# A six-layer graph-attention kernel: layer 1's input transposed into a bank of layer 0, its full copy placed behind the soft maximum

## The reference, cut to what matters

```python
# layer 0
q, k, v = x @ Wq + bq, x @ Wk + bk, x @ Wv + bv          # 8 heads of 32
attn = softmax(where(adj == 0, -inf, q k^T * scale))
x = layernorm((attn v) @ Wo + bo + x) * gamma + beta
# layer 1
sc = where(adj == 0, -inf, (x @ Wq) (x @ Wk)^T / 16)
x = layernorm(x + (softmax(sc) (x @ Wv)) @ Wo + bo) * gamma + beta
# layers 2 to 5
s = where(adj == 0, -1e10, (x Wq^T + bq) (x Wk^T + bk)^T / sqrt(128))
x = layernorm(x + (softmax(s) x) Wc^T) * g + b
```

## Time and profile before

| what | value |
|---|---|
| median of 3 runs | 2370.72 us (2369.71 to 2372.63) |
| the profiled execution | 2373.87 us, of which the span from first to last instruction is 2372.1 us |
| PE busy | 2259.9 us, 95% of the span |
| VectorE, ScalarE, GpSimd busy | 75%, 68%, 76% |
| granted TensorE clock | 0.99 of full |

### The profile page before, as it was taken

The page is one execution under the profiler, slowest core; times in us unless marked ns, Lnnn a source line. Parts: engine busy times, 40 slices in busy tenths (PEclk is TensorE's granted clock), DMA queues, the critical chain, the costliest instruction groups (busy, mean ns, idle before and its releaser), DMA issues.

```text
span 2372.1 us, 59576 instructions
## 1 busy us (share of the span) xinstructions
PE 2259.9 (95%) x20624; PEld 2136.2 (90%) x20624; DVE 1783.3 (75%) x7734; ACT 1620.0 (68%) x5515; POOL 1794.9 (76%) x2399
## 2 busy tenths in 40 slices
PE   6899999999999999999999999999999999999985
PEld 5799999999999999999999999999999999999974
DVE  4777777777877877877877877877777777777864
ACT  5667767767767767767767767766766766767742
POOL 3368878878878878878878878878878878878751
PEclk9999999999999999999999999999999999999998
DMA  4000000100110000010010000000010010000000
GB/s 154 20 23 24 30 28 24 30 28 25 29 28 25 29 28 26 28 28 26 28 28 27 27 28 28 26 28 28 26 28 28 26 28 28 26 29 17 15 10 14
DMA packets 38747, 68.78 MB, mean 29 GB/s; under 512 B 4400, under 2 KB 12848, under 8 KB 37936
## 3 DMA queue, kind: packets, MB, share of 16 engines
q1 hardware_dynamic: 38448, 64.97, 9.0%
HBM read 48.18 MB, written 16.78 MB: 27 GB/s over the span
## 4 chain that ended last, share of the span: by engine, by line
PE 80%; DVE 9%; ACT 7%; issue 2%; POOL 1%; DMA 0%; POOLq 0%; SPq 0%; DVEq 0%
PE value_bank L450 17%; PE qk_bank L442 16%; PE context_bank L595 9%; PE unit_bank L450 7%; PE unit_bank L442 7%; PE qk_bank L549 7%; PE score_bank L579 5%; ACT probs L676 5%; PE unit_bank L506 4%; PE unit_bank L518 3%; DVE scores L820 2%; PE score_bank L576 2%; PE score_bank L586 2%; DVE xT_lo L854 2%; DVE scores L860 1%
## 5 line engine op out<-in xcount | busy, mean ns | idle before, releaser
L1046 POOL TENSOR_TENSOR x<-y,rows 128x512 f32<-128x512 f32 x305 | 392.0, 1285 | 188.9 <-DVE y L913 188.9
L698 ACT CAST xT_hi<-qk_bank 128x512 fp32r<-128x512 f32 x320 | 187.7, 587 | 399.8 <-PE qk_bank L549 399.6
L676 ACT ACTIVATE probs<-scores,negmax 128x128 f32<-128x128 f32 x1024 | 399.1, 393 | 88.6 <-DVE negmax L820 88.6
L913 DVE TENSOR_SCALAR y<-y,mv,rstd 128x256 f32<-128x256 f32 x730 | 304.2, 459 | 191.6 <-POOL rstd L1030 191.3
L442 PE MATMUL qk_bank<-xT_hi,w_lo 128*128 128x256 f32 x1280 | 411.5, 321 | 21.6 <-DVE xT_lo L854 21.3
L1054 POOL TENSOR_TENSOR x<-x,rows 128x512 f32<-128x512 f32 x305 | 393.8, 1291 | 19.2
L450 PE MATMUL value_bank<-w_lo,xT_hi 128*128 128x256 f32 x1280 | 394.4, 308 | 0.0
L442 PE MATMUL qk_bank<-xT_lo,w_hi 128*128 128x256 f32 x1280 | 363.5, 284 | 0.0
L442 PE MATMUL qk_bank<-xT_hi,w_hi 128*128 128x256 f32 x1280 | 362.1, 283 | 0.0
L450 PE MATMUL value_bank<-w_hi,xT_lo 128*128 128x256 f32 x1280 | 361.8, 283 | 0.0
L450 PE MATMUL value_bank<-w_hi,xT_hi 128*128 128x256 f32 x1280 | 361.0, 282 | 0.0
(11 more groups left out here) (93 smaller groups left out, 6503.3 us busy)
## 6 DMA issues: line engine op xcount, KB each, us to landing
x0T<-xT_in SPq DMA_DIRECT2D x64, 256.0 KB, 3.0
x<-x_in SPq DMA_DIRECT2D x64, 256.0 KB, 3.0
out<-x_out SPq DMA_DIRECT2D x64, 256.0 KB, 2.3
adj<-adj_in SPq DMA_DIRECT2D x64, 128.0 KB, 2.2
late_weights<-w_in SPq DMA_DIRECT2D x2, 1024.0 KB, 7.1
rows<-rows_in SPq DMA_DIRECT2D x1, 1792.0 KB, 11.7
probs0T<-w_in SPq DMA_DIRECT2D x4, 256.0 KB, 4.2
x<-w_in SPq DMA_DIRECT2D x1, 1024.0 KB, 13.2
```

Source lines behind the costliest of these rows:

```text
L676: e = act.activation(probs0[:, j, g, quad], scores0[:, j, g, quad], ACT.Exp, scale=-1.0, bias=negmax0[:, j, g, quad:quad + 1], accum_out=t ...
L913: m = dve.tensor_scalar(y[:, r, g], y[:, r, g], mv[:, r, g, 0:1], rstd[:, r, g:g + 1], ALU.subtract, ALU.mult)
L1046: pool.tensor_tensor(result(norm), y[:, NORM_AT[norm] % YS], row_of_each(f"gamma{layer}"), ALU.mult).then_inc(zg_ready, 1)
```

## The change

Layer 1's x (of every group but group 0) is transposed into `unit_bank[0]` in place of `qk_bank`. TensorE waits there for `row_max0(g+1, 0)` and no longer for `move_qk(5g-1)`. ScalarE's full copy `xT` becomes a step of its own, `move_xT`, behind `softmax(5g-1)`, and waits until `xT_lo` is made; VectorE's `split_lo` waits for `xT_hi` alone. `project_qk(5g)` gets a wait for `qk_ready` of the item before, and `transpose_probs0(., 0)` one for the full copy.

```diff
--- before.py
+++ after.py
@@ -371,6 +371,10 @@
             else:
                 engine.wait_ge(x_ready, RESULT_AT[norm] + 1)
 
+        def xT_bank(i):
+
+            return unit_bank[0] if item(i)[0] == 1 and NTH[i] > 0 else qk_bank
+
         block = ctx.enter_context(nc.Block())
 
         @block.sync
@@ -501,6 +505,9 @@
                 if group == 0 and j == 0:
                     pe.wait_ge(eye_loaded, 16)
                 pe.wait_ge(probs0_ready, after_unit(group, j))
+                if j == 0 and group > 1:
+
+                    pe.wait_ge(xT_ready, group)
                 for g in range(G):
                     for quad in range(QUADS):
                         t = pe.transpose(unit_bank[j][:, (g * QUADS + quad) * N:(g * QUADS + quad + 1) * N],
@@ -542,11 +549,14 @@
             def transpose_x(i):
                 layer, group = item(i)
                 wait_result(pe, source_of(i))
-                if NTH[i] > 0:
+                psum = xT_bank(i)
+                if psum is not qk_bank:
+                    pe.wait_ge(negmax0_ready, after_unit(min(group + 1, GROUPS - 1), 0))
+                elif NTH[i] > 0:
                     pe.wait_ge(qk_ready, NTH[i])
                 for kd in range(KD):
                     for g in range(G):
-                        t = pe.transpose(qk_bank[:, (kd * G + g) * N:(kd * G + g + 1) * N],
+                        t = pe.transpose(psum[:, (kd * G + g) * N:(kd * G + g + 1) * N],
                                          x[:, group % HELD, g, kd * P:(kd + 1) * P], eye[:, :])
                 t.then_inc(xT_in_psum, 1)
 
@@ -554,6 +564,10 @@
                 layer, group = item(i)
                 parts = [("scores1", 0), ("scores1", P)] if layer == 1 else [(f"wqT{layer}", 0), (f"wkT{layer}", 0)]
                 pe.wait_ge(xT_lo_ready, after(i))
+                if xT_bank(i) is not qk_bank:
+                    pe.wait_ge(qk_ready, NTH[i])
+                elif layer == 1:
+                    pe.wait_ge(xT_ready, group + 1)
                 project(qk_bank, xT_hi[:, ring(i)], xT_lo[:, ring(i)], parts).then_inc(qk_in_psum, 1)
 
             def project_v(i, g):
@@ -695,9 +709,12 @@
                 act.wait_ge(xT_in_psum, after(i))
                 if NTH[i] >= RING:
                     act.wait_ge(v_in_psum, after(i) - RING)
-                act.copy(flat3(xT_hi[:, ring(i)]), qk_bank[:, :]).then_inc(xT_hi_ready, 1)
-                if layer == 1:
-                    act.copy(flat3(xT[:, :]), qk_bank[:, :]).then_inc(xT_ready, 1)
+                act.copy(flat3(xT_hi[:, ring(i)]), xT_bank(i)[:, :]).then_inc(xT_hi_ready, 1)
+
+            def move_xT(i):
+
+                act.wait_ge(xT_lo_ready, after(i))
+                act.copy(flat3(xT[:, :]), xT_bank(i)[:, :]).then_inc(xT_ready, 1)
 
             def move_qk(i):
                 layer, group = item(i)
@@ -756,6 +773,8 @@
                         split_first(name)
                 if item(i - 1):
                     softmax(i - 1)
+                if item(i) and item(i)[0] == 1:
+                    move_xT(i)
                 if item(i - 1) and late_values(i - 1):
                     move_v(i - 1)
                 if (group := due(i, 6)) is not None:
@@ -845,13 +864,8 @@
                 dve.reciprocal(rtotal[:, small(i)], total[:, small(i)]).then_inc(rtotal_ready, 1)
 
             def split_lo(i):
-                layer, group = item(i)
-                if layer == 1:
-
-                    dve.wait_ge(xT_ready, group + 1)
-                else:
-                    dve.wait_ge(xT_hi_ready, after(i))
-                dve.tensor_tensor(flat3(xT_lo[:, ring(i)]), qk_bank[:, :], flat3(xT_hi[:, ring(i)]).bitcast(F32),
+                dve.wait_ge(xT_hi_ready, after(i))
+                dve.tensor_tensor(flat3(xT_lo[:, ring(i)]), xT_bank(i)[:, :], flat3(xT_hi[:, ring(i)]).bitcast(F32),
                                   ALU.subtract).then_inc(xT_lo_ready, 1)
 
             def row_max(i):
```

## The result

The changed kernel takes 2356.62 us (median of 4 runs, 2355.78 to 2359.72) against 2371.68 (2369.71 to 2373.13): ratio 0.9939, 95% interval 0.9922 to 0.9957. That is 15 us less, 0.24 us for each of 62 groups. Forecast were 9.3 us and 0.15. The sign and the range of 2354 to 2370 held. The narrower range of the forecast itself, 2358 to 2364, was missed: the size was too small by more than a third.

What follows compares the result with a forecast made beforehand. TensorE, busy 95% of the span, was taken as the bound. `xT_lo` starting earlier gave 62 x 0.15 = 9.3 us, other terms nothing: 2370.7 - 9.3 = 2361.4 us; range 2354 to 2370, the forecast's own 2358 to 2364.

Steps and rivals of the forecast that it cites:

- The stall and what was awaited: TensorE's transposes of layer 1's x: x comes 0.50 us before `kT`, so only that much of the stall can go.
- The scores' start: `score(5g-1)` on TensorE, waiting for `kT`, starts at about 1205.48 in place of 1205.94: 0.46 us won per group.
- `xT_lo`'s start: On VectorE, `xT_lo` starts at row_max's end, 1207.10 in place of 1207.25: 0.15 us per group.
- Which of them decides: At `project_qk(5g)`, `xT_lo` sets the gain, 0.15 us per group; the other 0.3 becomes a TensorE wait.
- PE's own path: From the scores to `project_qk(5g)`, TensorE alone could start at 1207.33, winning up to 0.66 us per group.
- The moved copy costs nothing: ScalarE's list behind `softmax(5g-1)` runs 0.48 us later, but slack and idle times absorb it: cost set at nothing.
- The slack: Behind the moved copy, `xT_hi(5g+1)` has 0.06 us to spare before `xT_lo(5g+1)` must start to keep the gain.
- Rival 3: Slower: moved copy delays `xT_hi(5g+1)` on ScalarE; 0.9 us lateness costs 12 us, giving 2383 us. Chance 8%.
- Rival 1: The whole stall at the transposes goes: 0.46 to 0.66 us per group, 29 to 41 us, 2330 to 2342. Chance 5%.
- the rule on banks: Skill's advice to rotate matmul groups through PSUM banks; by it alone the transposes' whole stall, 48.7 us, would go.
- The new waits of TensorE: Added waits in `project_qk(5g)`, `transpose_probs0` and the context: cost zero, at most 0.10 us if one falls on `xT_lo`.

Runs made afterwards that it cites:

- exp_halves: Changed kernel, with ScalarE taking two of the four exponentials of `exp0(g+1, 0)` only after q, k and `probsT` of slot 5g-1: 2356.31 us.
- lo_first: Changed kernel, with VectorE making `xT_lo` of layer 1 ahead of `row_max` of the item before: 2414.86 us.
- bank_only: Changed kernel, with the full copy put back directly behind `xT_hi` and `xT_lo` waiting for it; only the new bank stays: 2352.58 us.
- wait_kept: Changed kernel, with layer 1's transposes in the new bank also waiting for `qk_ready`, as before the change: 2364.28 us.
- copy_late: Changed kernel, with one extra copy of `xT` into a spare tile on ScalarE, behind `move_probsT` in slot 5g: 2381.09 us, ratio 1.0030 to the kernel before.
- copy_twice: Changed kernel, with a second full copy of the bank, into a spare tile, in `move_xT`: 2408.16 us, ratio 1.0159 to the kernel before.

## Why the prediction was right, and where its size was off

**The stall and what was awaited: right.** x came 0.5 us before `kT`, and the transposes start 0.1 us after GpSimd (1195.92 + 1.29 = 1197.21, transposes at 1197.27). With x where it is, no more of that stall can go.

**The scores' start: mis-sized, 0.46 against 0.23.** The prediction let the scores wait for `kT` alone. `score` waits for `probsT` of the item before as well, which ScalarE makes directly behind `kT`. That wait had been hidden under the transposes, so the list of before has it 4 times with 1.4 us in total; the code shows it (`probsT_ready` in `score`), and so does the row of the timeline before that stands behind `kT`:

```profile
1205.23 0.36 ACT L727 COPY probsT<-score_bank 128x256 f32<-128x256 f32 x1
```

It ends at 1205.59, and the scores start 0.12 us behind it after the change, at 1205.71 in the clock of before. It is the wait that took the place of the one removed.

**`xT_lo`'s start: mis-sized, 0.15 against 0.36.** Two things were misread. `xT_lo` starts when row_max's last read of the accumulator starts, not when it ends: after the change both rows stand at 1199.30. Taking the end, 1207.10, for the start, 1207.02, made 0.08. And `row_max(5g-1)` was taken to hang on `normalise` alone, so as not to move. In fact the scores ended at 1205.94 + 0.61 = 1206.55 before, and row_max started 0.04 us behind that:

```profile
1206.59 0.29 DVE L860 CUSTOM_DVE_ANT_0 scores<-score_bank,mask 128x128 f32<-128x128 f32 x1
```

With scores 0.23 earlier it hung on `normalise` and came 0.12 to 0.13 earlier. `exp_halves` bears this out: there the scores come another 0.36 us earlier, and `xT_lo` stays where it is.

**Which of them decides: wrong, and the errors partly cancelled.** The sum had PE waiting 0.3 us for `xT_lo`. Measured, PE doesn't wait there: it comes to `project_qk` without a stop at the moment at which `xT_lo` is ready, 0.36 us earlier than before, and has gained 0.28 behind its first matmul. The term for PE's own path was too large (0.66, with scores 0.46 earlier), that for `xT_lo` too small (0.15), and the gain lies between the two terms. That the range held although the wait which was to set the gain isn't there is in part luck. `exp_halves` shows that `xT_lo` would be the limit directly behind: of 0.36 us at the scores 0.07 were left. `lo_first` shows that PE's own side is the other: `xT_lo` 0.42 us earlier brought `project_qk` nothing. `bank_only` shows that the bank alone brings everything, which the sum had the other way round (it took its 0.15 from the copy's place). `wait_kept` splits the 15 us: 6 for `xT_lo` no longer awaited, 9 more for the earlier transposes.

**The moved copy costs nothing: right within the noise, by a margin that was small.** Without the move (`bank_only`) the kernel is 2.7 us faster, if anything. `xT_hi(5g+1)` ends at 1205.56, 0.13 ahead of `xT_lo(5g+1)`, and VectorE's reciprocal waits 0.24, which its idle time covers. The slack was put at 0.06 and at about as much for VectorE; 0.46 us more cost 53 us. Rival 3 had priced 0.9 us of lateness of `xT_hi(5g+1)` at 12 us more than before. `copy_late` has about that lateness on this path alone and is 7 us slower than its before. The doubled copy has it on `exp0(g+1, 1)` too and is 37 us slower: rival 3 had not seen the path through VectorE, which is the dearer one.

**Rival 1** fell as argued, and so did the 48.7 us that the prediction drew from the rule on banks: the bank was one of several things awaited, and the new bank brought 15 of 48.7 us. **The new waits of TensorE** cost nothing: `xT_lo`'s end to `project_qk` is 0.06 us. **The first groups:** group 5 starts 0.5 to 1.7 us later in the profiles after, which the sum didn't have; by what `wait_kept` and `copy_twice` show of the scatter of this start, it can't be told from none.

## What to carry to other kernels

When a stall is removed, list every semaphore that the next instruction waits for, in the code and not in the profile: a wait that was fulfilled during the stall has hardly a row, and here it was the one that showed. Ask of each instruction on the new path whether it starts where it does because of its own engine or because of its input, since the input may move too. And work that is put into an engine's list where it has no idle time delays what others need further on: here a copy of 0.46 us, once too many, cost 0.85 us a group.

## What the runs showed of the hardware that was not expected

VectorE's `normalise` of two 128x256 tiles took 0.73 us alone, 1.22 to 1.31 us where it began with GpSimd's multiplication of 128x256 tiles (up to 0.16 us behind it), and 1.99 us where it began 0.62 us behind. One tile took 0.41 us alone. The rows tile by tile (medians) say why the later start cost more. In the changed kernel the first tile took 0.62 us and ended 0.15 us behind GpSimd's first multiplication, the second took 0.70 and ended 0.15 behind GpSimd's second. With the copy doubled the first tile took 0.71 us and ended 0.15 behind GpSimd's second multiplication, and the second tile ran beside the addition of beta that follows it, which takes 1.31 us: it took 1.36 and ended 0.15 behind that. So each tile ended with the GpSimd instruction that was under way, and the late start met the longer one.

The Trainium skill (SBUF — State Buffer, SBUF: two separate sides) has one port pair that a GpSimd instruction, or a VectorE instruction in a two-port mode or with two SBUF inputs, locks for its whole length, while the other blocks. The rows agree with that, 1.36 us against 0.41 beside an instruction of 1.31; in which mode `normalise` ran they don't show.

The same twelve matmuls of a layer-0 projection run at two paces. Timelines of PE in the kernel before, second and last matmul of one projection in two neighbouring periods:

```profile
1184.86 0.28 PE L442 MATMUL unit_bank<-x0T_hi,w_hi 128*128 128x256 f32 x1
...
1185.99 0.28 PE L442 MATMUL unit_bank<-x0T_lo,w_hi 128*128 128x256 f32 x1
```

```profile
1220.33 0.28 PE L442 MATMUL unit_bank<-x0T_hi,w_hi 128*128 128x256 f32 x1
...
1221.51 0.28 PE L442 MATMUL unit_bank<-x0T_lo,w_hi 128*128 128x256 f32 x1
```

Ten steps take 1.13 us in one and 1.18 in the other, at the same granted clock. Of these projections 70 of 112 were slow in the first profile of the kernel before, 15 of 112 in the second, and 10 of 113 after the change. These are the two kinds of period: in the first profile of before the 35 long periods of groups 5 to 60 hold two slow projections each, and the 21 short ones none. At 0.14 us a period the two profiles of before so differ by some 4 us. Profiles of other kernels here had 8 of 113 (`bank_only`), 15 (`wait_kept`) or 81 (`exp_halves`). What chooses the pace stays open, and with one profile of each it can't be said whether the kernel has a part in it.
